# Graph attention over a sparse adjacency: two of 128 half-tile loads leave eight partitions out, and their rows come in pieces over all DMA engines

## The reference

```python
h = jnp.maximum(_layernorm(x, axis=-1), 0.0)          # x: 8192 x 128
s_i = h @ attn[:d]
s_j = h @ attn[d:]
e = leaky_relu(s_i + s_j.T, negative_slope=0.2)
e = e + jnp.where(adj > 0, 0.0, -1e9)                 # adj: 8192 x 8192, int32
out = x + softmax(e, axis=1) @ h
```

## Time and profile before

| what | us |
|---|---|
| median of 3 runs | 822.78 (821.7 to 823.1) |
| span of the profiled execution | 819.9 |
| DMA share of the chain that ended last | 76% |
| busy: PE 379.5, DVE 615.3, ACT 534.3, POOL 505.0 | of 819.9 |
| last sign of the stream starts at | 746.96 |

### The profile page before, as it was taken

The page is one execution under the profiler, slowest core; times in us unless marked ns, Lnnn a source line. Parts: engine busy times, 40 slices in busy tenths (PEclk is TensorE's granted clock), DMA queues, the critical chain, the costliest instruction groups (busy, mean ns, idle before and its releaser), DMA issues.

```text
span 819.9 us, 6412 instructions
## 1 busy us (share of the span) xinstructions
PE 379.5 (46%) x1378; PEld 171.4 (21%) x1378; DVE 615.3 (75%) x2028; ACT 534.3 (65%) x410; POOL 505.0 (62%) x526
## 2 busy tenths in 40 slices
PE   1546334444444344344343434444434546653765
PEld 1322011111111011111111101111111215431654
DVE  6898298677768667797778666697689799897831
ACT  4975676676676666766766666676676677764620
POOL 6720777755457767665547677555557667655771
PEclk9776665555555555555555555655555556766768
DMA  8999999999999999999999999999999999981210
GB/s 341 402 411 415 392 404 408 406 414 413 409 407 410 408 405 410 406 410 410 412 406 407 408 406 407 411 410 413 412 413 409 408 411 407 409 348 43 53 37 4
DMA packets 39719, 301.59 MB, mean 368 GB/s; under 512 B 10682, under 2 KB 17149, under 8 KB 22272
## 3 DMA queue, kind: packets, MB, share of 16 engines
q1 hardware_dynamic: 24032, 277.04, 83.1%
q0 software_dynamic: 15360, 23.88, 8.5%
q10 hardware_dynamic: 288, 0.26, 0.1%
HBM read 303.76 MB, written 8.98 MB: 381 GB/s over the span
## 4 chain that ended last, share of the span: by engine, by line
DMA 76%; issue 11%; DVE 5%; ACT 4%; PE 3%; POOL 0%; DVEq 0%; ACTq 0%
DMA adj_ring<-in_adj_dram 75%; ACT sign_ring L613 3%; PE words L1442 2%; DVE one_hot L724 1%; ACT h_all L625 1%; PE words L1406 1%; DMA x_all<-in_x_dram 1%; PE words L1366 0%; DVE cand L769 0%; DVE adj_ring L1142 0%; DVE adj_ring L1138 0%; DVE adj_ring L1146 0%; PE words L1516 0%; POOL out_dram L562 0%; ACT terms L620 0%
## 5 line engine op out<-in xcount | busy, mean ns | idle before, releaser
L613 ACT ACTIVATE sign_ring<-adj_ring,half_neg 128x4096 fp8e3<-128x4096 int32 x128 | 474.9, 3710 | 217.1 <-DMA adj_ring<-in_adj_dram 215.4
L521 POOL DMA_INDIRECT near<-h_table,near_id x384 | 391.8, 1020 | 235.4 <-issue 122.8
L1366 PE MATMUL words<-sign_ring,pack_w 128*128 128x512 bf16 x512 | 225.2, 592 | 354.8 <-ACT sign_ring L613 354.8
L769 DVE MAX8 cand<-words 128x8 f32<-128x256 f32 x256 | 90.9, 417 | 115.4 <-PE words L1366 115.4
L1366 PEld LDWEIGHTS words<-sign_ring,pack_w 128*128 128x128 bf16 x512 | 55.0, 127 | 521.9 <-ACT sign_ring L613 451.6
L954 DVE TENSOR_REDUCE sums<-terms 128x128 f32<-128x1024 f32 x58 | 112.2, 1934 | 2.0
L532 POOL DMA_INDIRECT near_m<-h_table,id_m x64 | 64.5, 1008 | 19.5 <-issue 19.2
L949 DVE TENSOR_TENSOR terms<-near,weight 128x512 f32<-128x512 f32 (+1 forms) x87 | 73.4, 871 | 0.0
L1357 PE MATMUL words<-place,place_w 128*128 128x512 bf16 x128 | 62.1, 586 | 3.6 <-DVE key L861 3.6
L1392 PEld LDWEIGHTS listing<-cand,one_hot 128*128 128x128 f32 x128 | 33.6, 321 | 10.9 <-issue 7.7
L1347 PE MATMUL listing<-h_all 128*1 128x128 f32 x128 | 19.1, 322 | 22.8 <-ACT h_all L625 22.8
(11 more groups left out here) (271 smaller groups left out, 524.3 us busy)
## 6 DMA issues: line engine op xcount, KB each, us to landing
adj_ring<-in_adj_dram SPq DMA_DIRECT2D x128, 2048.0 KB, 24.6
near<-h_table,near_id POOLq DMA_INDIRECT x384, 6.4
h_table<-h_all POOLq DMA_DIRECT2D x4, 1056.0 KB, 14.7
x_all<-in_x_dram SPq DMA_DIRECT2D x4, 1024.0 KB, 9.4
out_dram<-x_all SPq DMA_DIRECT2D x30, 128.0 KB, 23.9
near_m<-h_table,id_m POOLq DMA_INDIRECT x64, 6.4
out_dram<-x_all ACTq DMA_DIRECT2D x2, 128.0 KB, 2.5
adj_ring<-h_table SPq DMA_DIRECT2D x1, 132.0 KB, 2.6
```

What stands on the lines that cost most here:

```text
L521: pool.indirect_dma_start(out=near[:, p % RING, k, :], out_offset=None, in_=table, in_offset=bass.IndirectOffsetOnAxis(ap=near_id[:, p % I ...
L613: nc.scalar.activation(bytes_of, adj_ring[:, n % HALVES, :].rearrange("p (d r i) -> p d r i", r=2, i=WORDS), ACT.Sign, bias=half_neg[:, :] ...
L769: last = nc.vector.max(out=cand[:, p % 2, t % 2, 8 * q:8 * q + 8], in_=words[t % 3][:, q * PART:(q + 1) * PART])
L1366: last = nc.tensor.matmul(at[:, k * BANK:(k + 1) * BANK], pack_w[:, d, :], twins[:, o + k * BANK:o + (k + 1) * BANK], start=False, stop=(d ...
```

## The change

Two halves, n = 44 (pair 9's entry in `APART` is 4 * 9 + 8) and n = 80 (pair 18), are no longer loaded by SP. For each of them:

- ACT, right after the sign of half n - 5, waits for its own count and issues eight DMAs, one for each partition in 12 to 15 and 44 to 47: a 16 KB row of the half, cut in 16 pieces of 1 KB (`load_rows_apart`).
- POOL, ahead of the gathers of pair 9 (or 18), waits until these eight have landed, and then issues one indirect DMA that brings the other 120 rows (`load_apart`); the numbers in `half_id` are out of bounds for the eight partitions, so nothing is fetched for those.
- ACT's sign of that half waits for the indirect DMA (`half_in`) in place of SP's. The counts that the other halves of a buffer are waited for by are one lower from there on (`whole_loads`).

At the start POOL makes `half_id` with two iotas and eight selects that wait for each other, behind the wait for the table's stores. `seat`, made with five iotas among the constants, takes the place of `entry` in the lists: the first 120 places of a list are the partitions other than the eight, the last 8 places are the eight.

```diff
+    RELIEVED = ((12, 16), (44, 48))
+    SPREAD = 16
+    APART = {9: 4 * 9 + 8, 18: 4 * 18 + 8}
+    APART_ROWS = sum(b - a for a, b in RELIEVED)
...
+    def whole_loads(n):
+        return sum(m not in APART.values() for m in range(n % HALVES, n + 1, HALVES))
...
+    adj_halves = adj.rearrange("r (h c) -> (r h) c", h=2)
...
             def load_pair(p):
                 for n in range(4 * p, 4 * p + 4):
+                    if n in APART.values():
+                        continue
                     if n >= HALVES:
                         sp.wait_ge(signed, n - HALVES + 1)
...
+            at = 0
+            held = P - APART_ROWS
+            for low, high in zip((0,) + tuple(b for a, b in RELIEVED), tuple(a for a, b in RELIEVED) + (P,)):
+                nc.gpsimd.iota(seat[:, low:high], pattern=[[1, high - low]], base=at - int(FAR), channel_multiplier=0,
+                               allow_small_or_imprecise_dtypes=True)
+                at += high - low
+            for low, high in RELIEVED:
+                nc.gpsimd.iota(seat[:, low:high], pattern=[[1, high - low]], base=held - int(FAR), channel_multiplier=0,
+                               allow_small_or_imprecise_dtypes=True)
+                held += high - low
...
+            for i, n in enumerate(APART.values()):
+                nc.gpsimd.iota(half_id[:, i:i + 1], pattern=[[0, 1]], base=n, channel_multiplier=2 * TILES) \
+                    .then_inc(half_id_done, 1)
+            pool.wait_ge(half_id_done, len(APART))
+            passes = len(APART)
+            for low, high in RELIEVED:
+                for r in range(low, high):
+                    nc.gpsimd.affine_select(out=half_id[:, :], in_=half_id[:, :], compare_op=ALU.not_equal,
+                                            fill=float(4 * N), base=-r, pattern=[[0, len(APART)]],
+                                            channel_multiplier=1).then_inc(half_id_done, 1)
+                    passes += 1
+                    pool.wait_ge(half_id_done, passes)
+
+            def load_apart(p):
+                n = APART[p]
+                i = list(APART).index(p)
+                pool.wait_ge(apart_in, 16 * APART_ROWS * (i + 1))
+                pool.indirect_dma_start(
+                    out=adj_ring[:, n % HALVES, :], out_offset=None, in_=adj_halves,
+                    in_offset=bass.IndirectOffsetOnAxis(ap=half_id[:, i:i + 1], axis=0),
+                    bounds_check=last_half, oob_is_err=False).then_inc(half_in, 16)
...
+                if p in APART:
+                    load_apart(p)
                 gather_pair(p)
...
-                    act.wait_ge(adj_in[n % HALVES], 16 * (n // HALVES) + 16)
+                    if n in APART.values():
+                        act.wait_ge(half_in, 16 * list(APART.values()).index(n) + 16)
+                    else:
+                        act.wait_ge(adj_in[n % HALVES], 16 * whole_loads(n))
...
+                    if n + HALVES in APART.values():
+                        load_rows_apart(n + HALVES)
+
+            def load_rows_apart(n):
+                act.wait_ge(signed, n - HALVES + 1)
+                cols = slice((n % 2) * HALF, (n % 2 + 1) * HALF)
+                for low, high in RELIEVED:
+                    for r in range(low, high):
+                        act.dma_start(
+                            adj_ring[r:r + 1, n % HALVES, :].rearrange("p (k c) -> p k c", k=SPREAD),
+                            adj_t[n // 2, r:r + 1, cols].rearrange("p (k c) -> p k c", k=SPREAD)).then_inc(apart_in, 16)
...
-                    nc.vector.tensor_scalar(one_hot[:, p % 2, a, :], entry[:, :], key[:, 2 * p + a:2 * p + a + 1],
+                    nc.vector.tensor_scalar(one_hot[:, p % 2, a, :], seat[:, :], key[:, 2 * p + a:2 * p + a + 1],
```

More of the change, by code:

```diff
@@ L135, in graph_attention_kernel @@
         entry = sb("entry", [P, P], fp32)
+        seat = sb("seat", [P, P], fp32)
+        half_id = sb("half_id", [P, len(APART)], i32)
         code_mask = sb("code_mask", [P, CHUNKS], i32)
@@ L294, in graph_attention_kernel @@
         consts = sem("consts")
+        half_id_done = sem("half_id_done")
+        apart_in = sem("apart_in")
+        half_in = sem("half_in")
         near_zeroed = sem("near_zeroed")
@@ L512, in _ @@
             last_row = pool.to_reg(N - 1)
+            last_half = pool.to_reg(2 * N - 1)
+            for i, n in enumerate(APART.values()):
[18 more added lines that the diff above has]
+                    bounds_check=last_half, oob_is_err=False).then_inc(half_in, 16)
             pool.sem_inc(far_free, 1)
```

## The result

The changed kernel takes 826.6 us (median of 4 runs, 826.03 to 827.78) against 822.36 for the kernel before on the same chip: ratio 1.0056, 95% interval 1.0042 to 1.007. The prediction was 814.7 us and faster. The profiled execution has a span of 824.3 us and a time of 826.03. All medians and ratios here are of runs in the fast state; two slow runs (833.52 us of three_swap, 1315.31 of groups_swap) are left out.

What follows compares the result with a forecast made beforehand. The adjacency stream was taken to be bound by one lagging DMA engine of sixteen. -9.0 of lag and +0.9 of pieces gave -8.1, span 819.9 to 811.8; with 2.9 for the median, 814.7 us, range 812.0 to 819.5.

Steps and rivals of the forecast that it cites:

- What bounds the kernel: Adjacency stream's end: one of sixteen DMA engines lags by about 9.0 us; relieving its eight partitions gives -9.0.
- Rival C: DVE's dense stretch cannot start earlier, so only its waits give, 4.3 us: 818.5 us; chance 0.15.
- D: Stream's end: the lag is larger, 12.0 us, so the relief itself is the bound: 812.3 us; chance 0.07.
- more work for the others: All engines: 16 pieces of 1 KB each over both halves, 0.65 to 1.2 us, taken as 0.9.
- The pieces' landing: Eight row DMAs beside the stream: 11 us taken, between 7.9 and 13.4; upper bound 33.7 if one after the other.
- POOL's wait: POOL before pair 9's gathers: they start at 266, 7 us late, hidden by DVE's 11.3 us of room; no cost.
- rival B: Both loads queue and land too late: +14, 837 us; DMA share below 0.9 around 300 or 510; chance 0.06.
- The indirect load: POOL's 120 rows, issued near 265, land at 273 to 279; half 44's sign by 281; no cost.
- ACT's issues: Eight issues behind the sign of half 39: 3.1 us, caught up one or two halves later; nothing, twice.
- The start: POOL's iotas and eight selects, 3.6 us, delay the first gather; nothing, or at the worst 1 us.
- The list places: Gathers of lists: eight partitions filled last save the lagging engine up to 8 us, taken as 2; moves no end.
- Rival A: Another engine lags, so it gets extra pieces and nothing off: +0.9, 823.7 us; chance 0.12.

Runs made afterwards that it cites:

- three_swap: groups_swap with six rows a half (12 to 14, 44 to 46) apart, by two DMAs of three rows, list places unchanged; 818.84 us, ratio 0.9969.
- groups_swap: swap_whole with the eight rows of a half brought by two DMAs of four rows; 819.29 us, ratio 0.9966.
- Relief: The changed kernel with the eight partitions' rows not brought at all (stale data) and POOL waiting only for the buffer; 813.25 us, ratio 0.9907.
- swap_whole: The changed kernel with POOL's load first, once the buffer is free, then the whole rows after it landed; only ACT waits for them; 824.95 us, ratio 1.003.
- late: Relief with POOL's load held back until three more halves are signed, still without the rows; 816.05 us, ratio 0.9913.
- pool_all: The changed kernel with POOL's indirect DMA bringing all 128 rows of both halves once the buffer is free, ACT issuing nothing; 816.37 us, ratio 0.9942.
- groups: The changed kernel with a half's eight rows brought by two DMAs of four rows instead of eight of one row; 819.29 us, ratio 0.9976.
- lists: The kernel before with only the new order of list places; all halves loaded by SP; 818.44 us, ratio 0.997.

## Why the prediction was wrong, point by point

- **What bounds the kernel** was right: one engine lagging by about 9 us, and its eight partitions. Relief gives -8.4 us by the medians, -7.6 by the ratios, against the -9.0 of that term; the tail follows it. Rival C (DVE takes part) is refuted by it, and so is D. But the list places would have given 3.3 of it without any relief.
- **The step that failed is "more work for the others"**, the 0.9 us for pieces that all engines share. The rows came as 16 packets of 16 KB, all on one engine: 10.9 us on it by the arithmetic, and 10.1 to 11.7 measured by swap_whole with what the late half costs. The warning was already there: the listing of ACT's order shows the eight DMAs as `1x4096`, a single run, and not as 16 x 256. Both sides of the copy are contiguous, so the cut written in the code is no cut. That the change does not do what it says should have been a rival, and it alone would have given the other sign: +10.9 in place of +0.9 is +1.9 us, near 825.
- The Trainium skill ("DMA: Bandwidth & Descriptors", Why a DMA increments its semaphore by 16 and not by 1) states that the number of engines is the largest up to 16 that divides the slowest dimension that isn't 1 on both sides, that software can split a contiguous row so that it goes over all of them, and that DMAs from SP or ACT on fewer than 16 engines take the lowest-numbered ones. The packet counts agree with the first part for 16 pieces, four rows and three rows (16, 4 and 3 completions a DMA: 1024, 32 and 24 packets more). For a whole row the rule taken by its words, with a dimension of 4096, would give 16 engines; the trace shows one completion a DMA, and rows 2.4 us apart. The split that the code wrote didn't reach the DMA. No run names the engine of a packet.
- **The pieces' landing** was taken to end near 265; it ended at 273.87. The wide bound of 33.7 held it. The reason for 11, that another queue's packets do not stand behind SP's whole backlog, still holds with a row every 2.4 us, but it was worked out for one packet an engine, and here eight went in a row on one.
- **POOL's wait** was priced at nothing. Two signs that the prediction had named are there: the share falls to 0.84 in 292 to 296 and 0.71 in 480 to 484 (rival B's sign), and pair 9's gathers start at 276.45, where it had said by 268. By the starts of the last sign, -8.1 of relief and +10.9 of rows are +2.8, where the change has +3.85: 1 us is left for the wait. By the times, relief and swap_whole's rows together are +3.3 by the medians, where the change is +4.2, and +2.5 by the ratios, where it is +4.6: 1 to 2 us are left. The wait is the smaller mistake.
- **The indirect load** lands 15.4 us after its issue, over the 8 to 14 that I gave it. Half 44's sign starts at 289.31, not by 281. With the rule of rival B, nothing is lost up to 295. But the change's windows from 280 to 296 are short of 1.9 us of stream against 409 GB/s, and those of late, with the sign at 284.28, have 374, 396 and 385 GB/s. The room was less than I made it.
- **ACT's issues** took 2.60 us, not 3.1, and cost nothing seen. **The start**: relief has it too, and meets the sum. **The list places** were said to move no end; alone they start the last sign 3.5 us earlier.
- **Rival A** comes nearest to the time (823.7) and has the right picture, a low share as long as before, but for the wrong reason: the relieved engine was the right one, and the rows made a new laggard.

## What to carry to other kernels

When a stream is bound by the engine with the most bytes, ask for every DMA that is added how many engines it runs on, and read that from the built access pattern and the packet count, not from the way the slice is written. A few rows in one DMA cost far less than the same rows in a DMA each: in ACT's time (0.87 us against 2.60), in landing, and in balance. And before repairing a laggard with a new transfer, look for work that can simply be moved off it: the list places gave 3.3 us for five small instructions. An experiment that leaves something out also needs the kernel that leaves nothing out but is otherwise the same beside it. Against the kernel before, relief looks like 8.4 us for eight partitions; against pool_all it is 3.1.

## What I had not expected of the hardware

- **Small transfers can slow the stream while all engines look busy.** Two DMAs of four 16 KB rows, 128 KB in all, come with 270 to 286 GB/s over 4 us at a share of 0.93 to 1.08. In three_swap it is 313 and 232 GB/s in two such windows, though only six rows move. The eight rows' packets take 9.1 us in groups and 6.3 in the change. The cause is open.
- **One DMA of 16 pieces costs ACT 0.65 us to issue** (10.45 for 16), twice that of a whole row (2.60 for 8, 0.33).
- **A 2 MB load by POOL's queue lands 14.5 to 14.9 us after its issue** in pool_all, while SP's loads need 24.6. That it does not stand behind their backlog is the likely reason, but not shown.

Left open: where pool_all's 2 us over lists come from; a row in 16 pieces by one DMA, and POOL's load in flight together with the rows, weren't tried.
